# Second cross attention: value sums by query, with the exponentials as the stationary operand

## The reference

```python
q, k, v = x, ctx, ctx                    # (2,512,512), (2,1024,512)
# 16 heads of width 32
scores = einsum('bhqd,bhkd->bhqk', qh, kh) / sqrt(32)
scores = where(ki <= qi + 512, scores, -10000)     # query qi sees keys up to qi + 512
attn = softmax(scores)
out = einsum('bhqk,bhkd->bhqd', attn, vh)
x = layernorm(x + out)
```

## Time and profile before

| | us |
|---|---|
| median of three runs | 2269.06 (2265.43 to 2271.65) |
| the profiled execution's own time | 2268.35 |
| its span in the profile | 2266.3 |
| PE / DVE / ACT / POOL busy over the whole span | 1987.9 / 1448.3 / 1079.4 / 602.4 |
| preparation of the second cross attention, first DMA to first score tile | 1560.87 to 1610.96 |
| its 32 heads, to the last product of `output` | 1610.96 to 1877.24 |
| next phase begins | 1891.26 |

### The profile page before, as it was taken

One profiled execution on the slowest core, in us unless ns is written; L12 is line 12 of the kernel. 1 busy time (PEld: TensorE's weight loads), 2 busy tenths in 40 slices (PEclk: granted clock), 3 DMA queues, 4 the chain that ended last, 5 costly groups with the idle time before them and its releaser, 6 DMA issues. The chain is left out here.

```text
span 2266.3 us, 32930 instructions
## 1 busy us (share of the span) xinstructions
PE 1987.9 (88%) x11168; PEld 1193.0 (53%) x11168; DVE 1448.3 (64%) x2728; ACT 1079.4 (48%) x2150; POOL 602.4 (27%) x510
## 2 busy tenths in 40 slices
PE   7888878969999799977999999996698886799998
PEld 4555544447777477753545445452355543355553
DVE  5666666376775577765848566577699965555334
ACT  4666634232334233332726355471898893345332
POOL 3555500032331333300101001011645450123220
PEclk8999988988999799998999999997799997999999
DMA  4000003020110211004110010004600003466533
GB/s 137 25 25 1 1 18 136 1 72 28 43 46 1 71 47 46 23 0 137 38 38 21 22 52 0 1 1 87 158 1 2 1 1 114 156 175 191 137 71 89
DMA packets 95792, 125.26 MB, mean 55 GB/s; under 512 B 8926, under 2 KB 52254, under 8 KB 95662
## 3 DMA queue, kind: packets, MB, share of 16 engines
q1 hardware_dynamic: 88942, 107.79, 15.7%
q0 software_dynamic: 6720, 15.73, 3.8%
HBM read 101.68 MB, written 18.61 MB: 53 GB/s over the span
## 5 line engine op out<-in xcount | busy, mean ns | idle before, releaser
L1170 POOL TENSOR_TENSOR wl<-stage,wh 128x512 fp32r<-128x512 f32 x80 | 117.3, 1498 | 395.2 <-DVE wh L1161 395.2
L1429 POOL TENSOR_TENSOR Zl<-z,Zh 128x512 f16<-128x512 f32 x32 | 51.1, 1598 | 493.8 <-ACT Zh L1590 493.8
L77 PE MATMUL PS<-XTh,wh 128*128 128x512 f16 x416 | 160.0, 385 | 19.8 <-ACT t L2013 19.0
L1270 ACT ACTIVATE h<-PS,bup 128x512 f32<-128x512 f32 x64 | 44.2, 690 | 277.9 <-PE PS L79 277.9
L78 PE MATMUL PS<-XTl,wh 128*128 128x512 f16 x416 | 159.6, 384 | 0.0
L79 PE MATMUL PS<-XTh,wl 128*128 128x512 f16 x416 | 159.4, 383 | 0.0
L2476 POOL TENSOR_TENSOR PTl<-P,PTh 128x512 f16<-128x512 f32 (+2 forms) x128 | 116.4, 920 | 124.3 <-ACT PTh L2648 124.2
L2647 ACT ACTIVATE P<-PS 128x512 f32<-128x512 f32 (+3 forms) x256 | 135.1, 528 | 21.6 <-PE PS L2573 19.8
L2648 ACT ACTIVATE PTh<-PS 128x512 f16<-128x512 f32 (+3 forms) x256 | 136.2, 532 | 0.0
L2663 DVE TENSOR_REDUCE M<-PS 128x1 f32<-128x640 f32 (+3 forms) x128 | 127.1, 1012 | 4.5 <-PE PS L2549 4.5
L2476 DVE TENSOR_TENSOR PTl<-P,PTh 128x512 f16<-128x512 f32 (+1 forms) x128 | 96.1, 756 | 50.0 <-ACT PTh L2648 48.7
(11 more groups left out here) (378 smaller groups left out, 5872.0 us busy)
## 6 DMA issues: line engine op xcount, KB each, us to landing
stage<-in_ffn_W SPq DMA_DIRECT2D x18, 1024.0 KB, 5.4
stage<-in_ffn_Wg SPq DMA_DIRECT2D x9, 1024.0 KB, 5.5
stage<-in_ffn_Wup SPq DMA_DIRECT2D x16, 512.0 KB, 3.9
stage<-in_ffn_Wdn SPq DMA_DIRECT2D x16, 512.0 KB, 3.6
wq<-in_attn_wq SPq DMA_DIRECT2D x4, 1024.0 KB, 5.9
C<-in_ctx SPq DMA_DIRECT2D x8, 512.0 KB, 8.9
stage<-in_ffn_Wsw SPq DMA_DIRECT2D x16, 256.0 KB, 3.5
stage<-in_attn_WV SPq DMA_DIRECT2D x16, 256.0 KB, 4.1
```

The source lines that it names most:

```text
L77: pe.matmul(out, a[0], b[0], start=start, stop=False, skip_group_check=True)
L1170: nc.gpsimd.tensor_tensor(piece(wl[q], ch), piece(st, ch), plain(piece(wh[q], ch)), ALU.subtract).then_inc(w_lo, 1)
```

## The change

The roles of the operands in the value product are swapped. A block of 128 keys by 128 queries of the exponentials is stationary, and columns of `V` move: 33 columns (high part and ones), 32 columns (low part), and 33 again for the low part of the exponentials. So the sums come out with queries on the partitions, 33 numbers for each of four query tiles. They alternate between banks 6 and 7. The copy `Zs`, the matrix `comb` and the combining product go; DVE reads the sums from PSUM at kt = 2. The maxima of a group are turned with one transpose (16 stationary columns), and the shift is made on 16 partitions by 128. The float32 ring `P32` has 6 buffers and the float16 ring 13. The heads of a group now lie next to each other in `QS` and `KS`.

```diff
-    SLOTS = 4
-    RING = CT + 4
+    SLOTS = 6
+    RING = CT + 5
+    ZW = DV + 1
...
+        def z_bank(n):
+            return c.PS[:, 6 + n % 2, 0:QT * ZW].rearrange("p (q e) -> p q e", q=QT)
+        def turned_bank(n):
+            return c.PS[0:GS * QT, 6 + n % 2, QT * ZW:QT * ZW + P]
...
-                sp.dma_start(QS[b][R:R + 1, h4::4, :], mh[:]).then_inc(m_in, 16)
+                sp.dma_start(QS[b][R:R + 1, h4 * GS:(h4 + 1) * GS, :], mh[:]).then_inc(m_in, 16)
...
-            def turn_maxima(g):
+            def turn_maxima(g, n):
                 pe.wait_ge(max_done, QT * GS * (g + 1))
-                need(pe, z_out, GS * (g + 1) - LEAD - 1)
-                for qt in range(QT):
-                    last = pe.transpose(c.PS[0:GS, 7, qt * P:(qt + 1) * P], M[:, b, qt, h:h + GS], c.ident[:])
+                need(pe, z_out, n - 1)
+                pe.transpose(turned_bank(n), M[:, g].rearrange("p j q -> p (j q)"), c.ident[:]).then_inc(m_turned, 1)
...
             def value_tile(n, kt):
                 if kt == 0:
-                    need(pe, z_copied, n)
-                pe.matmul(c.PS[0:VW, 6, cols], v, PTh[:, slot, cols], start=(kt == 0), stop=False, ...)
-                last = pe.matmul(c.PS[0:VW, 6, cols], v, PTl[:, slot, cols], start=False, ...)
+                    need(pe, z_out, n - 1)
+                    pe.wait_ge(m_shift, 1 + sum(turn_group(i) is not None for i in range(n + 1)))
+                for qt in range(max(kt - K0, 0), QT):
+                    q = slice(qt * P, (qt + 1) * P)
+                    pe.matmul(z_bank(n)[:, qt, :], PTh[:, slot, q], v[:, DV:VW], start=(kt == 0 and qt == 0), ...)
+                    pe.matmul(z_bank(n)[:, qt, 0:DV], PTh[:, slot, q], v[:, 0:DV], start=False, ...)
+                    last = pe.matmul(z_bank(n)[:, qt, :], PTl[:, slot, q], v[:, DV:VW], start=False, ...)
-            def combine(n):
...
         # ACT
-            for n in range(N + 2):
-                if n >= 2:
-                    act.wait_ge(z_done, CT * (n - 1))
-                    nc.scalar.activation(Zs[:, n % 2, :], c.PS[0:VW, 6, :], ACT.Copy).then_inc(z_copied, 1)
-                if n == N:
-                    for t in range(QT):
-                        norm.root(act, t)
+            for n in range(N):
...
-            for t in range(QT, NT):
+            for t in range(NT):
                 norm.root(act, t)
         # DVE
-                    if kt == 4 and n >= 2:
+                    if kt == 2 and n >= 2:
                         output(n - 2)
```

More of the change, by code:

```diff
@@ L2538, in max_tile @@
             def max_tile(n, qt):
-                b, h, _ = head(n)
+                b, _, h = head(n)
                 i = QT * n + qt
@@ L2550, in max_tile @@
                           skip_group_check=True).then_inc(s_done, 1)
-            def turn_maxima(g):
-                b, h = divmod(GS * g, H)
+            def turn_maxima(g, n):
                 pe.wait_ge(max_done, QT * GS * (g + 1))
-                need(pe, z_out, GS * (g + 1) - LEAD - 1)
-                for qt in range(QT):
-                    last = pe.transpose(c.PS[0:GS, 7, qt * P:(qt + 1) * P], M[:, b, qt, h:h + GS], c.ident[:])
-                last.then_inc(m_turned, 1)
+                need(pe, z_out, n - 1)
+                pe.transpose(turned_bank(n), M[:, g].rearrange("p j q -> p (j q)"), c.ident[:]).then_inc(m_turned, 1)
             def exp_tile(n, kt):
-                b, h, _ = head(n)
+                b, _, h = head(n)
                 i = CT * n + kt
@@ L2580, in value_tile @@
                 if kt == 0:
-                    need(pe, z_copied, n)
-                cols = slice(first_query(kt), S)
+                    need(pe, z_out, n - 1)
+                    pe.wait_ge(m_shift, 1 + sum(turn_group(i) is not None for i in range(n + 1)))
                 v, slot = V[:, b * CT + kt, h, :], (CT * n + kt) % RING
[L2584 to L2587, removed]
-                last.then_inc(z_done, 1)
-            def combine(n):
[L2591 to L2597, removed]
+                for qt in range(max(kt - K0, 0), QT):
+                    q = slice(qt * P, (qt + 1) * P)
+                    pe.matmul(z_bank(n)[:, qt, :], PTh[:, slot, q], v[:, DV:VW], start=(kt == 0 and qt == 0), stop=False,
+                              skip_group_check=True)
+                    pe.matmul(z_bank(n)[:, qt, 0:DV], PTh[:, slot, q], v[:, 0:DV], start=False, stop=False,
+                              skip_group_check=True)
+                    last = pe.matmul(z_bank(n)[:, qt, :], PTl[:, slot, q], v[:, DV:VW], start=False,
+                                     stop=(kt == qt + K0), skip_group_check=True)
+                last.then_inc(z_done, 1)
             pe.wait_ge(const_done, 2)
-            pe.wait_ge(const_in, 48)
+            pe.wait_ge(const_in, 32)
             for n in range(LEAD):
@@ L2604, in _ @@
                 if n == GS:
-                    turn_maxima(0)
+                    turn_maxima(0, 0)
             pe.wait_ge(ones_done, 2)
             pe.wait_ge(v_lo, B * CT)
-            for n in range(N + 2):
+            for n in range(N + 1):
                 for kt in range(CT):
@@ L2613, in _ @@
                         max_tile(n + LEAD, kt // 2)
-                    if 1 <= n <= N:
+                    if n >= 1:
                         value_tile(n - 1, kt)
-                    if kt == 3 and n >= 2:
-                        combine(n - 2)
                     if kt == 5 and turn_group(n) is not None:
-                        turn_maxima(turn_group(n))
+                        turn_maxima(turn_group(n), n)
             if not norm.to_dram:
@@ L2631, in _ @@
             act.wait_ge(v_lo, B * CT)
-            for n in range(N + 2):
-                if n >= 2:
-                    act.wait_ge(z_done, CT * (n - 1))
-                    need(act, c_done, n - 3)
-                    nc.scalar.activation(Zs[:, n % 2, :], c.PS[0:VW, 6, :], ACT.Copy).then_inc(z_copied, 1)
-                if n == N:
-                    for t in range(QT):
-                        norm.root(act, t)
-                for kt in range(CT if n < N else 0):
+            for n in range(N):
+                for kt in range(CT):
                     i = CT * n + kt
@@ L2658, in max_tile @@
             def max_tile(n, qt):
-                b, _, h = head(n)
                 i = QT * n + qt
```

51 lines of the change are left out of this document (23 added, 28 removed).

## The result

| | before | changed | forecast |
|---|---|---|---|
| median on one chip, us | 2268.86 (4 runs) | 2241.32 (2237.43 to 2247.47, 4 runs) | 2242 |
| ratio, 95% interval | | 0.9882 (0.9854 to 0.9910) | 0.988 |
| profiled execution's own time, us | 2268.35 | 2239.3 | 2241.5 |
| span, us | 2266.3 | 2237.5 | |

The change saved 27.5 us, 1.2%. The time lies 0.7 us from the forecast, but that is partly luck: the terms were off by up to 2.4 us, with both signs, and one of the reasons was wrong. The four runs of the changed kernel alone lie up to 10 us apart.

The account below looks back on a forecast made before the run. A loop through PE, ACT and DVE, closed by the single bank and ACT's copy, bounded the turns with maxima. Savings of 19 + 3.8 + 2 + 0.5 + 1.6 = 26.9 us gave 2242 us, range 2234 to 2262.

Parts of the forecast that it names:

- What bounded the kernel before: Turns with maxima: a loop through PE, ACT and DVE, closed by the single bank and ACT's copy; 19 us less.
- Narrow products: PE's value products: 78 a turn at 28 ns, 2.2 us; PE falls from 7.26 to 5.85 us a plain turn.
- rival 3: PE's value products: loads not hidden; PE has 8.27 us a turn at 59 ns a pair, 2336 at 89 ns; chance 0.05.
- "DVE ... more than ACT's 6.7": Turns with maxima: DVE at 7.3 us a turn exceeds ACT's 6.7 and PE's 5.85; 24 x 7.3 = 175.2 us.
- DVE's work in four turns: Turns with maxima: DVE's own work falls from 30.03 to 28.8 us in four turns, the shorter shift saving 1.2.
- Moments: DVE's queue between turns 20 and 23: four tiles at about 1.08 us count in full, 4.3 us.
- Wait for `m_shift`: PE's value product, once in four turns: priced at nothing, or 0.5 us in four turns at the upper end.
- Turns without maxima: Last six turns, bounded by ACT: 6.7 us each instead of 7.33, 3.8 us less, between 3 and 5.5.
- rival 4: PE granted 1.2 GHz because it has less work: 9.8 us a turn, total 2300; chance 0.06.
- Preparation: POOL's sixteen low parts before the turns: six buffers remove part of the pauses; 2 us less, between 0 and 3.1.
- End: Last outputs, no longer behind copies and combining products: last output 1.6 us earlier, between 1 and 3.
- The signs that were named: DVE busy at least 95%, turns with maxima 7.1 to 7.5 us, without 6.4 to 6.8, narrow products 25 to 31 ns apart.

Follow-up runs that it names:

- e3: Kernel before, with one transpose of a group's maxima, the shift on 16 partitions and the new order of heads; 2263.58 us, ratio 0.9979.
- e1: Changed kernel with four float32 buffers instead of six; 2243.14 us, ratio 0.9877.
- e5: Changed kernel with eight more PE products of 252 columns in each turn with maxima, into columns nobody reads; 2248.04 us, ratio 0.9898.
- e4: Changed kernel with all value sums in bank 6, turned maxima in bank 7 and output at the start of a turn; 2312.43 us, ratio 1.0188.
- e7: Changed kernel with the low part of key tile 5 on POOL instead of DVE; 2236.36 us, ratio 0.9841.
- e8: Changed kernel with DVE's moments of batch 0 moved from turns 20 to 23 to turns 26 to 29; 2237.10 us, ratio 0.9841.
- e2: e3 with five float32 buffers instead of four; 2263.53 us, ratio 0.9978.
- e12: Changed kernel itself, unaltered, measured again on another chip; 2243.61 us, ratio 0.9874.

## Why the prediction was right, and where its reasons were not

- **What bounded the kernel before: right, by exclusion.** The shift alone gives 5 us (e3), the buffers nothing in the turns (e1), and PE's saved work is nearly all slack in the new turn (e5). What is left is the loop over the single bank and ACT's copy. A loop over one bank, closed through DVE, costs 70 us (e4). Which part of the gain is the second bank's and which the copy's, the runs do not separate.
- **Narrow products: right.** Taken at 28 ns, measured 25 to 26. The 31 ns taken for a load are the spacing of loads and not their length, which is 96 ns in both places; the loads overlap. PE has 6.09 us in a plain turn, where 5.85 were forecast; 6656 columns at 0.21 us for 512 are 2.7 us and not 2.8, and rival 3's sum is 8.25 and not 8.27, which changes nothing. Rival 3 is out.
- **ACT: right** (6.7 taken, 6.67 measured).
- **"DVE ... more than ACT's 6.7": wrong for plain turns.** This step took DVE's full queue as the bound of all turns. e7 takes 0.8 us from DVE and the plain turn stays at 6.94: ACT with its late score tile sets it, and DVE's 6.80 lies just under that. In the turns with the shift and with moments DVE is late, and they shrink when it has less to do (e7, e8). The size came out nearly right because two errors cancel. Plain turns were 0.36 us shorter than the 7.3 taken, and the turns with the shift 0.4 to 1.1 us longer. The 20 turns without moments average 7.20 us, (177.16 - 33.26)/20.
- **DVE's work in four turns** was taken as 30.03 - 1.2 = 28.8 us. It is 7.51 + 3 x 6.80 = 27.9. The shift saved what was forecast. Of the other 0.9 us the twelve full low parts give 0.4 (0.72 us each before, 0.69 now, one of 0.91 among them before); the rest is overlap, since operations that follow without a gap overlap by 0.08 us in the records.
- **Moments: right** (4.3 taken; 33.26 - 3 x 6.94 - 7.72 = 4.7 found, two stretches at half clock included; e8 shows that it goes with them).
- **Wait for `m_shift`: right in kind, but not free.** It was priced at nothing. PE waits there 6.8 us in 7 waits over the stage, up to 1.1 at a time, and in each of the six turns with a shift from 3 to 23 ACT then waits 0.68 to 0.75 us for its second score tile. That is nearly the whole 0.78 by which such a turn is longer than a plain one. The shift's own 0.76 us on DVE fits as well. In e7 both go together: DVE is early, PE's wait falls from 6.6 to 0.2 us and the excess is gone. No run drops this wait from the code, so whether it or DVE's full queue holds those turns is open.
- **Turns without maxima: 3.8 us forecast, 1.9 found.** The mis-sized term is 6.7 us a turn. At full clock it is 6.81, and at the clock of 0.50 that came here 7.03. The 7.33 it was set against is high too: such a turn of the kernel before is 7.27, and the mean took in a longer first one. This is rival 4 in small: the clock did fall, but PE at 6.60 of 7.03 busy still lay beside ACT.
- **Preparation: 2 us forecast, 4.3 found.** I let the buffers remove part of POOL's pauses. They removed all of them: POOL's run went from 20.65 to 17.53 us, 3.1 less, which was the upper end of the range, and five buffers do as much as six (e2). The other 1.1 us is POOL's earlier start, which differs by 1.5 us among the traces without regard to the buffers.
- **End: 1.6 us forecast, 2.4 found.** The range of 1 to 3 held it; which part of the chain gave the other 0.8 was not looked into.
- **The signs that were named.** PE's share, the narrow products and the lost copy came as named. Plain turns of 6.94 us lie below the 7.1 to 7.5, and turns without maxima (6.81 to 7.03) above the 6.4 to 6.8. The sign of rival 4, a clock of 0.50 in mid-stage, did come, four times for 3.4 us; in a turn with the shift it cost 0.6 us, far from the 1.5 a turn that the rival had.

Sum of the terms in the stage: 26.9 forecast, 30.2 found, less 1.4 that other phases gave back. With e12's trace in place of the first the stage gives 27.2.

## What to carry to other kernels

When no engine is full and each waits a little for the next, look for the buffer that closes the loop and give it a second copy, and take the link out of a busy engine's queue; PE's work given back cost a seventh of its length (e5), and taking the second bank away again costs 70 us (e4). Before calling an engine the bound because it is busy 98% of a turn, move a piece of its work away: if the turn stays, another path is as long, and the busy share may hardly fall, since waiting can count as busy, as on DVE here (e7). Work that comes only in some turns, such as a shift or the moments of a norm, belongs where the engine has room: the same moments some forty microseconds later were free (e8).

## What the hardware showed that I had not expected

- With a stationary operand of 128x128 float16 and 33 moving columns, a load and its product follow each other every 25 to 26 ns at full clock, 78 times a turn. The Trainium skill ("TensorE: Matmul & The Clock Gate", LDWEIGHTS) gives a load's time as its columns divided by 1.2 GHz, an estimate of 107 ns for these 128. The trace nearly agrees for one load, whose record is 96 ns, but the loads overlap, so that this is not their spacing. The list of lines of the changed kernel, 1640 to 1680 (count, busy us, mean ns):

```profile
L2589 PEld LDWEIGHTS PS<-V,PTh 128*128 128x128 f16 x151 | 13.2, 96 | 3.3 <-issue 1.4
```

- At a granted clock of 0.50 the same products stand 28 to 30 ns apart, not twice 25. PE's timeline of the changed kernel:

```profile
1692.77 0.19 PE L2589 MATMUL PS<-V,PTh 128*128 128x33 f16 x1
1692.80 0.19 PE L2591 MATMUL PS<-V,PTh 128*128 128x32 f16 x1
...
1692.86 0.19 PE L2589 MATMUL PS<-V,PTh 128*128 128x33 f16 x1
```

- The clock fell to half in the middle of a steady stage, for 3.4 us at 1633.8, 1691.8, 1770.3 and 1787.4, while PE was busy 6.1 of 6.9 us in the plain turns around it, and for 34.1 us at 1811.3, behind a turn with PE busy 4.84 of 6.81. The kernel before shows none between 1621 and 1881, with PE busy 7.26 of 7.96; e3, whose plain turns are the same, shows one of 6.8 us at 1809.1.
- In e4, with PE waiting 2.6 us at a time, the clock fell again and again: 0.82 and 0.67 over whole turns.
